# Local attention's window softmax in a two-layer vision kernel: exponentials straight from PSUM on ScalarE, one instruction per unit of 60 keys

## The reference

```python
out = conv2d(x, conv1_w, conv1_b, PAD); out = instance_norm(out); out = leaky_relu(out)
out1 = conv2d(out, conv2_w, conv2_b, PAD)
mask = sigmoid(conv2d(out, mask_w, mask_b, PAD))
xm = out * mask
q, k, v = 1x1 convolutions of xm (k and v of xm padded by 1)
sims = [sum_c(q * k[:, :, i:i + H, j:j + W]) for i in range(3) for j in range(3)]
attn = softmax(stack(sims, axis=-1), axis=-1)
out2 = sum of attn[..., idx] * v[:, :, i:i + H, j:j + W] over the 9 neighbours
return residual + out1 * mask + (1.0 - mask) * out2
```

## Time and profile before

| | us |
|---|---|
| device time, median of 3 runs | 212.4 |
| lowest and highest run | 212.31 and 212.72 |
| span of the profiled execution, first to last instruction | 210.1 |
| PE, DVE, ACT, POOL busy in it | 184.5, 161.3, 119.4, 70.5 |

### The profile page before, as it was taken

How to read it: one execution, slowest core, us unless ns; L and a number is a source line. 1 busy time by engine, 2 the same in 40 slices (tenths; PEclk the granted TensorE clock), 3 DMA queues, 4 the chain that set the end, 5 groups by cost and what they waited for, 6 DMA issues and landing times.

```text
span 210.1 us, 5374 instructions
## 1 busy us (share of the span) xinstructions
PE 184.5 (88%) x2158; PEld 104.0 (50%) x2167; DVE 161.3 (77%) x382; ACT 119.4 (57%) x251; POOL 70.5 (34%) x62
## 2 busy tenths in 40 slices
PE   1799879879986999899997999899799998899972
PEld 1349339333353756643576455743423345565741
DVE  6798799988768859599497986994928576992682
ACT  2175273655259461967692862775845583966850
POOL 7600803150310403660007613750044003670290
PEclk9999999978999999999999999999999999999998
DMA  6412031001501000001000040001001000000002
GB/s 199 80 57 58 2 100 50 3 0 37 163 0 50 3 5 10 3 3 39 0 3 0 3 147 13 6 3 46 4 6 47 3 0 10 8 5 8 5 2 103
DMA packets 10154, 6.75 MB, mean 32 GB/s; under 512 B 7248, under 2 KB 8496, under 8 KB 10128
## 3 DMA queue, kind: packets, MB, share of 16 engines
q1 hardware_dynamic: 9888, 5.82, 10.2%
q10 hardware_dynamic: 240, 0.58, 0.7%
HBM read 3.30 MB, written 1.05 MB: 21 GB/s over the span
## 4 chain that ended last, share of the span: by engine, by line
PE 53%; DVE 22%; ACT 12%; issue 5%; DMA 3%; POOL 1%; SPq 1%; DVEq 0%; ACTq 0%
PE ps L1455 20%; PE ps L1375 5%; PE ps L1368 5%; PE ps L1402 5%; PE ps L1498 4%; ACT xw L703 3%; ACT p_t L720 3%; DVE sh_in L316 3%; PE ps L1533 3%; DMA w3b<-in_w_gi 2%; ACT sh_x L608 2%; PE ps L1544 2%; DVE ln_out L968 2%; PE ps L1522 2%; PE ps L1587 2%
## 5 line engine op out<-in xcount | busy, mean ns | idle before, releaser
L1455 PE MATMUL ps<-sh_ln,w_gi 96*64 96x512 f32 x192 | 44.6, 615 | 1.7 <-DVE sh_ln L316 1.7
L473 POOL TENSOR_TENSOR ln_s<-ln_s,neg_half 128x16 f32<-128x16 f32 x7 | 20.4, 2909 | 55.5 <-DVE ln_s L947 55.5
L608 ACT ACTIVATE sh_ln<-ln_out 32x512 f32<-32x512 f32 (+2 forms) x46 | 25.6, 557 | 14.6 <-DVE ln_out L968 5.5
L1455 PEld LDWEIGHTS ps<-sh_ln,w_gi 96*64 96x64 f32 x192 | 15.4, 140 | 25.9 <-issue 25.8
L1402 PE MATMUL ps<-w_qk,sh_ln 128*128 128x128 f32 x192 | 23.2, 278 | 0.4 <-issue 0.4
L1402 PEld LDWEIGHTS ps<-w_qk,sh_ln 128*128 128x128 f32 x192 | 22.2, 192 | 1.9 <-DMA sh_ln<-ln_out 0.9
L1498 PE MATMUL ps<-sh_in,w_in 96*32 96x256 f32 x384 | 22.8, 380 | 0.0
L1368 PE MATMUL ps<-busy 128*128 128x512 bf16 x68 | 19.4, 419 | 1.3 <-issue 1.2
L608 ACT ACTIVATE sh_x<-x 32x496 f32<-32x496 f32 (+1 forms) x20 | 12.3, 616 | 9.2 <-DVE x L1093 9.0
L1498 PEld LDWEIGHTS ps<-sh_in,w_in 96*32 96x32 f32 x384 | 11.9, 109 | 10.3 <-issue 3.0
L498 POOL TENSOR_TENSOR omm<-ones,msk 128x512 f32<-128x512 f32 x4 | 7.1, 1780 | 22.6 <-DVE msk L1169 22.6
(11 more groups left out here) (142 smaller groups left out, 334.6 us busy)
## 6 DMA issues: line engine op xcount, KB each, us to landing
sh_ln<-ln_out SPq DMA_DIRECT2D x27, 64.0 KB, 2.1
x_res<-in_x SPq DMA_DIRECT2D x4, 256.0 KB, 2.8
out_x<-out_s SPq DMA_DIRECT2D x4, 256.0 KB, 2.0
x_norm<-in_x SPq DMA_DIRECT2D x3, 256.0 KB, 2.9
kc<-in_shape_consts ACTq DMA_DIRECT2D x1, 450.0 KB, 4.9
w3b<-in_w_gi SPq DMA_DIRECT2D x1, 288.0 KB, 5.0
x_norm<-in_x SPq DMA_DIRECT2D x2, 128.0 KB, 2.8
xm<-xm SPq DMA_DIRECT2D x8, 25.5 KB, 1.9
```

The costliest lines, as they stand in the source:

```text
L473: nc.gpsimd.tensor_tensor(ln_s[n][:, 3, :], ln_s[n][:, 2, :], neg_half[:, :], ALU.pow)\
L608: return nc.scalar.activation(o, i, ACT.Copy)
L1455: mm = nc.tensor.matmul(ps[EC * h:EC * h + EC, GI_BANKS[n], :], w_gi[:, dy, n % 2, :], xs[:, n // 2, y:y + H // 2, 0:W], start=(dy == 0), ...
```

## The change

DVE no longer subtracts the maximum and no longer sums. It takes the maximum with its sign turned (`negate=True`). ScalarE reads the scores from PSUM, with one Exp for each unit of 60 keys, 8 for a half and 16 for a pair. Each has that unit's negated maximum as its per-partition bias (a pointer to `wsm[:, 0, u]`) and writes the sum of its results along the keys to `wsm[:, 1, u]` (`accum_out`). DVE keeps the reciprocal and the product. The steps on `window_softmax_steps` fall from 10 to 6 for a pair, and the waits are renumbered. TensorE's second convolution of the last pair, which overwrites a bank of scores of the pair before, waits for the exponentials in place of the subtraction.

```diff
--- before.py
+++ after.py
@@ -258,7 +258,7 @@
         g_k_sb = signal("k_in_sbuf", 2)
         g_v_sb = signal("v_in_sbuf", 2)
         g_s = signal("sims_in_psum", 2, start=1)
-        g_sm = signal("window_softmax_steps", 10)
+        g_sm = signal("window_softmax_steps", 6)
         g_we = signal("window_exp", 2)
         g_t = signal("probs_t_in_psum", 2, start=1)
         g_t_sb = signal("probs_t_in_sbuf", [4] * (PAIRS - 1) + [2], start=1)
@@ -705,11 +705,15 @@
                             xm[:, i, TH * a:TH * a + KH, TW * b:TW * b + KW], ACT.Copy)
                     ins.then_inc(g_xw.sem, 1)
 
-            def window_exp(pair):
+            def window_exp(pair, early=False):
                 for h in range(2):
-                    act.wait_ge(g_sm.sem, g_sm.at(pair, 2 * h + 2))
-                    pr = prob[:, UPB * h:UPB * h + UPB, 0:KEYS]
-                    nc.scalar.activation(pr, pr, ACT.Exp).then_inc(g_we.sem, 1)
+                    act.wait_ge(g_sm.sem, g_sm.at(pair, h + 1))
+                    for n in range(UPB):
+                        u = UPB * h + n
+                        ins = nc.scalar.activation(prob[:, u, 0:KEYS],
+                                                   ps[:, sims_bank(early) + h, KEYS * n:KEYS * n + KEYS], ACT.Exp,
+                                                   bias=wsm[:, 0, u:u + 1], accum_out=wsm[:, 1, u:u + 1])
+                    ins.then_inc(g_we.sem, 1)
 
             def probs_t(pair, early=False):
                 act.wait_ge(g_pv.sem, g_pv.before(pair))
@@ -831,7 +835,7 @@
             key_windows(last)
             probs_t(but_last)
             out1_evac(last, True)
-            window_exp(last)
+            window_exp(last, True)
             v_evac(last, True)
             pv_evac(but_last)
             probs_t(last, True)
@@ -1185,10 +1189,7 @@
                     units = slice(UPB * h, UPB * h + UPB)
                     sims = ps[:, sims_bank(early) + h, 0:UPB * KEYS].rearrange("p (u k) -> p u k", k=KEYS)
                     dve.wait_ge(g_s.sem, g_s.at(pair, h + 1))
-                    nc.vector.reduce_max(wsm[:, 0, units], sims, AX.X).then_inc(g.sem, 1)
-                    dve.wait_ge(g.sem, g.at(pair, 2 * h + 1))
-                    nc.vector.tensor_tensor(prob[:, units, 0:KEYS], sims, wsm[:, 0, units].unsqueeze(2)
-                                            .broadcast_to([P, UPB, KEYS]), ALU.subtract).then_inc(g.sem, 1)
+                    nc.vector.reduce_max(wsm[:, 0, units], sims, AX.X, negate=True).then_inc(g.sem, 1)
 
             def window_probs(pair):
 
@@ -1196,10 +1197,8 @@
                 for h in range(2):
                     units = slice(UPB * h, UPB * h + UPB)
                     dve.wait_ge(g_we.sem, g_we.at(pair, h + 1))
-                    nc.vector.reduce_sum(wsm[:, 1, units], prob[:, units, 0:KEYS], AX.X).then_inc(g.sem, 1)
-                    dve.wait_ge(g.sem, g.at(pair, 3 * h + 5))
                     nc.vector.reciprocal(wsm[:, 2, units], wsm[:, 1, units]).then_inc(g.sem, 1)
-                    dve.wait_ge(g.sem, g.at(pair, 3 * h + 6))
+                    dve.wait_ge(g.sem, g.at(pair, 2 * h + 3))
                     nc.vector.tensor_tensor(prob[:, units, 0:KEYS], prob[:, units, 0:KEYS], wsm[:, 2, units]
                                             .unsqueeze(2).broadcast_to([P, UPB, KEYS]), ALU.mult)\
                       .then_inc(g.sem, 1)
@@ -1568,7 +1567,7 @@
                 for t in range(UNITS // 2):
                     if t % 4 == 0:
                         pe.wait_ge(g_v_sb.sem, g_v_sb.at(pair, t // 4 + 1))
-                        pe.wait_ge(g_sm.sem, g_sm.at(pair, 3 * (t // 4) + 7))
+                        pe.wait_ge(g_sm.sem, g_sm.at(pair, 2 * (t // 4) + 4))
                     mm = nc.tensor.transpose(ps[:, values_banks(early)[t // 4], P * (t % 4):P * (t % 4) + P],
                                              prob[:, 2 * t:2 * t + 2, :].rearrange("p u k -> p (u k)"),
                                              kc[:, K_ID:K_ID + P])
@@ -1683,7 +1682,7 @@
             mask_conv(last, True)
             window_v(but_last)
             window_q(last, True)
-            pe.wait_ge(g_sm.sem, g_sm.at(but_last, 4))
+            pe.wait_ge(g_we.sem, g_we.done(but_last))
             conv2(last, True, images=(0,))
             window_k(last, True)
             probs_transposed(but_last)
```

## The result

The changed kernel takes 218.73 us (median of 6 runs, 215.87 to 219.49), the kernel before 212.53 (6 runs, 211.72 to 212.83). The ratio is 1.0259, 95% interval 1.0202 to 1.0316: it is slower, by about 5.5 us; the medians differ by 6.2, but the ratio leaves out two slow runs of the changed kernel. The prediction was 218.5 us, and slower with a chance of 0.92.

A forecast was written before the change was run, and what follows sets the result against it. TensorE held 53% of the chain, but at the program's end the softmax itself was on it. There +5.1 us, plus 1.0 for the clock, made span 216.2; with 2.3 above the span, 218.5 us, range 213.8 to 226.

The forecast's parts named there:

- The unit's cost s: ScalarE's time from one unit's exponential to the next one's start: 0.317 us, with 0.26 to 0.40 given 55%.
- a hidden write: Rival: the sum's write on ScalarE is hidden, s = 0.18 to 0.26, 214.0 to 217.5 us; chance 20%.
- one that awaits its exponential: Rival: no overlap at ScalarE's accumulator, s over 0.40, up to 0.51, 229.4 us there; chance 17%.
- Place 1: Pair `but_last`: the last pair's tanh and mask wait behind 16 exponentials, 16 s - 1.3 us late, 3.8 us.
- TensorE's new wait: TensorE's wait for both halves of exponentials costs nothing, since the tanh feeding its queries stands behind them anyway.
- Place 2: Pair `last` at the program's end: its last product moves by 16 s - 3.7 us, +1.4 us.
- Steps 0 and 1: Middle steps: exponentials stay covered up to s of 0.34 and 0.32, costing nothing; at 0.51 they add 2.7 and 3.0 us.
- The clock: TensorE's clock falls behind its longer gap ahead of the last queries: +1.0 us, bounds 0 and +1.8.
- The gap: TensorE's idle time of 0.4 us ahead of the queries of `last` grows by 3.8 us.
- The sum: Whole kernel: +5.1 us at the program's end and +1.0 for TensorE's clock, +6.1 us on the span, 218.5 us measured.
- the prediction's rival at s = 0.42: Case of no overlap at the accumulator: 8.4 + 1.2 + 1.5 = +11.1 us, 223.5 before the clock; rival's chance 17%.

The follow-up runs named there:

- tanh_k_first: Changed kernel with ScalarE's tanh of `last` ahead of `but_last`'s exponentials, and TensorE's keys ahead of its wait for them; ratio 1.0096 to the kernel before.
- tanh_first: Changed kernel with ScalarE's tanh of `last` moved ahead of the exponentials of `but_last`; ratio 1.0301 to the kernel before.
- place2_only: Kernel before with the changed softmax scheme for the pair `last` alone; ratio 1.0044 to the kernel before.
- steps_only: Kernel before with the changed softmax scheme for pairs 0 and 1 only; ratio 0.9984 to the kernel before.
- place1_only: Kernel before with the changed softmax scheme for the pair `but_last` alone; ratio 1.0305 to the kernel before.
- no_pointer: Changed kernel with an immediate scale of 0 in place of the bias pointer, accumulator kept, no valid softmax; one execution, 0.193 us a unit.
- wide_pool: Kernel before, softmax unchanged, with GpSimd's residual product of `last` made to wait for DVE's first product; ratio 0.9999 to the kernel before.
- half_last_pool: Kernel before with GpSimd's residual product of `last` made to wait for DVE's first, and the changed scheme for `last`'s second half; ratio 0.9968 to the kernel before.

## Why the prediction came out right

- **The unit's cost s.** Forecast 0.317 (0.26 to 0.40), measured 0.287. The parts were 0.207 for exponential and pointer (measured 0.193) and 0.11 for an overlapped small instruction (measured 0.094). As an instruction of its own the read was foreseen as a possibility, with no row behind it. The rivals of a hidden write and of one that awaits its exponential are both refuted by the rows of L713.
- **Place 1.** 16 s - 1.3 gives 3.3 us with the measured s; the mask came 3.5 late. The rest is the tanh, 0.06 us longer, and the mask's old start, which DVE's timeline has at 186.39 and not at 186.51. tanh_k_first confirms that the delay comes by way of the waits, and tanh_first that there are two of them. Here the prediction was incomplete: TensorE's new wait was costed at nothing, on the ground that the tanh covers it. That holds for the order of the changed kernel, but with the tanh moved away the wait costs about as much.
- **Place 2.** 16 s - 3.7 gives 0.9 us; measured 0.86 in place2_only and in the changed kernel.
- **Steps 0 and 1.** Costed at nothing below s = 0.32; shown by steps_only.
- **The clock.** Taken at 1.0 us, measured at 1.5 in the changed kernel and 2.8 in place1_only, the latter above my bound of 1.8. The two other falls in the end stretch cost 1.6 (tanh_first, no_pointer), so the term was too small in every trace that has one. The gap was foreseen (3.8 us and 0.4; measured 3.9).
- **The sum.** 3.3 or 3.5, 1.5 and 0.9 make 5.7 to 5.9 us, against 6.1 predicted: s was 10% too high (+1.0 us over both places) and the clock 0.5 too low, so two errors partly cancelled. That 218.5 lies 0.2 us from the measured median is luck beyond that. By the ratio the change costs 5.5 us, and the clock alone, a matter of the single execution, moves the end by 1.3 us between two traces. In the prediction's rival at s = 0.42 the steps are 1.3 + 1.6 and not 1.2 + 1.5; nothing hangs on it.

Left open: why tanh_first's ratio (1.0301) shows nothing of the 1.4 us that its profile gained over the changed kernel. Three of its four executions had a mean granted clock of 0.973 or 0.974, against 0.984 in the profiled one, so the clock fell for longer there; where, their traces would have to show. The same holds for the changed kernel's five executions that took 2.5 us more than the traced one and upwards: an early fall like that of before is worth 1.7 us of it. That the execution of before and the changed kernel differ in the early fall is likewise only observed.

## What to carry to other kernels

An in-order engine's spare time is not slack for whatever is queued behind the new work: look for the instruction right behind the insertion and for who waits for it. Here ScalarE was busy for 57% of the span before the change, and the 16 small instructions still cost 5 us, 3.5 by delay and 1.5 by the clock, since a tanh on the chain stood behind them; reordering took back 4.2 us in the traces. Splitting one wide instruction into 8 costs 8 times the fixed part, plus the pointer, plus the accumulator's read, and saves on another engine only what was on the chain there. When a slowed neighbour is moved away along with it, run the move without the change as well: here the move alone gave as much as both together (wide_pool and half_last_pool).

## What the runs showed of the hardware

- An exponential with a sum is two instructions on ScalarE, ACTIVATE and ACTIVATION_READ_ACCUMULATOR; in a row the read adds 0.094 us, though its own row is 0.19 to 0.30 us long. The pointer adds 0.094 as well.
- In a long run of such small instructions the rows grow (0.30 to 0.40 us at the last pair) while the starts stay 0.287 us apart: durations of overlapped instructions are no price.
- The granted clock is not settled by the idle time: behind 1.73 us it fell in one execution and not in another, behind 2.43 us it fell and behind 2.45 it did not, and behind 3.91 us it cost 1.5 or 2.8 us.
- DVE's product of two SBUF tiles takes 0.66 us alone and up to 1.65 us where one of GpSimd's 128x512 products began first. Where DVE's began first it took 0.66 us, and GpSimd's took 1.74 us in place of 1.27.
